# Three transfer edits in an attention-plus-dense kernel: first input block prepared one loop earlier, weight load cut into three, residual loads placed later

## The reference

```
x0: (4, 8192, 1024) float32
xn = layernorm(x0)
# attention part
k, v, q = fft(xn @ Wk.T + bk), fft(xn @ Wv.T + bv), fft(xn @ Wq.T + bq)
kv = cumsum(k * v, axis=1)
a = kv * conj(q);  a = a / (1e-9 + norm(a));  attn = real(ifft(a)) / sqrt(1024)
# dense part, with weights that are +1 or -1 (booleans k0, k1, k2)
h = concat([xn, -xn]) @ w0 * s0;  h = relu(h) * 2
h = h @ w1 * s1;                  h = relu(h) * 2
ffn = h @ w2 * s2
return x0 + attn + ffn
```

## Time and profile before

| what | us |
|---|---|
| median of 2 executions | 4095.31 (4073.11 and 4117.51) |
| profiled execution, device time | 4067.28 |
| its span, slowest core (7) | 4065.5 |
| spans of all cores | 4044.3 to 4065.5 |
| PE busy | 3647.6 (90%) |
| mean granted TensorE clock | 0.950 |

### The profile page before, as it was taken

The page is one execution under the profiler, slowest core; times in us unless marked ns, Lnnn a source line. Parts: engine busy times, 40 slices in busy tenths (PEclk is TensorE's granted clock), DMA queues, the critical chain, the costliest instruction groups (busy, mean ns, idle before and its releaser), DMA issues.

```text
span 4065.5 us, 43732 instructions; the slowest of 8 cores (4044.3 to 4065.5 us)
## 1 busy us (share of the span) xinstructions
PE 3647.6 (90%) x16512; PEld 1590.1 (39%) x16512; DVE 1119.8 (28%) x1586; ACT 1131.4 (28%) x1504; POOL 700.3 (17%) x842
## 2 busy tenths in 40 slices
PE   4658895898994999899899999989989998999998
PEld 1323331333331444344344444434434443444443
DVE  0034436687770111111211301111121111112112
ACT  3844442445553210311211031031112103112110
POOL 0022223455550002001100100100010010001001
PEclk9778897899997999999999999999999999999999
DMA  4143343544415344343434424334443443434343
GB/s 83 21 104 83 84 101 71 88 73 93 84 34 183 106 154 141 122 152 137 143 135 155 157 102 155 133 124 158 155 156 104 156 132 117 155 132 148 125 151 129
DMA packets 331198, 491.53 MB, mean 121 GB/s; under 512 B 217328, under 2 KB 219376, under 8 KB 297200
## 3 DMA queue, kind: packets, MB, share of 16 engines
q0 software_dynamic: 97632, 375.43, 28.2%
q1 hardware_dynamic: 219536, 71.36, 7.9%
q10 hardware_dynamic: 13824, 41.95, 2.8%
HBM read 276.87 MB, written 58.72 MB: 83 GB/s over the span
## 4 chain that ended last, share of the span: by engine, by line
PE 82%; DMA 5%; DVE 4%; issue 4%; ACT 3%; SPq 2%; POOL 0%; ACTq 0%; DVEq 0%; POOLq 0%
PE pd L962 44%; PE pd L661 13%; PE pd L918 11%; PE pd L1018 10%; PE pd L666 2%; PE pd L297 2%; DMA xn_f<-xn_dram 1%; SPq L533 1%; SPq L885 1%; DMA wtmp<-Wk 1%; DVE bx_t L1047 1%; PE pd L504 1%; DVE xn_t L482 1%; DMA xn_dram<-xn_t 1%; DMA w2ring<-k2u 1%
## 5 line engine op out<-in xcount | busy, mean ns | idle before, releaser
L962 PE MATMUL pd<-r_t,w1r 128*128 128x512 bf16 x8192 | 1769.4, 379 | 7.8 <-ACT r_t L932 7.8
L962 PEld LDWEIGHTS pd<-r_t,w1r 128*128 128x128 bf16 x8192 | 801.0, 98 | 976.2 <-issue 11.6
L980 DVE TENSOR_SCALAR w1r<-w1r 128x4096 bf16<-128x4096 bf16 x232 | 284.7, 1227 | 1830.2 <-DMA w1r<-w1s 1830.2
L918 PE MATMUL pd<-xn_f,K0d_t 128*128 128x512 bf16 x2048 | 460.2, 388 | 121.0 <-DMA xn_f<-xn_dram 57.0
L975 POOL DMA_DIRECT2D w1r<-w1s x232 | 125.7, 542 | 2095.5 <-PE pd L962 1830.3
L988 ACT ACTIVATE r_t<-pd,s_scales 128x512 bf16<-128x512 f32 x256 | 176.5, 689 | 1112.4 <-PE pd L962 1111.6
L1018 PE MATMUL pd<-w2ring,r_t 128*128 128x512 bf16 x2048 | 444.7, 379 | 12.3 <-ACT r_t L988 7.8
L918 PEld LDWEIGHTS pd<-xn_f,K0d_t 128*128 128x128 bf16 x2048 | 203.3, 100 | 377.9 <-issue 148.8
L1018 PEld LDWEIGHTS pd<-w2ring,r_t 128*128 128x128 bf16 x2048 | 199.1, 98 | 257.9 <-issue 21.3
L932 ACT ACT_TABLE_LOAD x64 | 82.1, 1283 | 615.0 <-DMA part_t<-partial_dram 506.6
L661 PE MATMUL pd<-xn_f,AkR 128*128 128x512 bf16 x512 | 144.4, 433 | 89.8 <-DMA xn_f<-xn_dram 77.8
(11 more groups left out here) (150 smaller groups left out, 2486.3 us busy)
## 6 DMA issues: line engine op xcount, KB each, us to landing
w1r<-w1s POOLq DMA_DIRECT2D x256, 1024.0 KB, 4.7
w2ring<-k2u POOLq DMA_DIRECT2D x256, 256.0 KB, 2.6
conv_t<-k0u POOLq DMA_DIRECT2D x64, 256.0 KB, 4.0
w1s<-k1u SPq DMA_DIRECT2D x32, 512.0 KB, 5.7
bx_t<-x_own ACTq DMA_DIRECT2D x32, 512.0 KB, 7.3
out<-bx_t ACTq DMA_DIRECT2D x32, 512.0 KB, 3.1
x_t<-x_extra POOLq DMA_DIRECT2D x8, 1024.0 KB, 9.4
k0s<-conv_o SPq DMA_DIRECT2D x32, 256.0 KB, 2.9
```

The source lines that it names most:

```text
L918: inst = te.matmul(reg.ap, K0d_t[:, dk * F0 + m * 128: dk * F0 + (m + 1) * 128], xn_f[fb][:, dk * TST:(dk + 1) * TST], start=(dk == 0), st ...
L962: inst = te.matmul(reg.ap, w1ring[c % 3][:, k * 128:(k + 1) * 128], r0_t[:, k * TST:(k + 1) * TST], start=(k == 0), stop=(k == NF0 - 1))
L980: lambda: v.tensor_scalar(w1ring[c % 3][:], w1ring[c % 3][:], 2.0, -1.0, op0=OP.mult, op1=OP.add))
```

## The change

Three edits, all of when and on which engine something is issued; no arithmetic changes.

1. The preparation of own block 0 is taken out of A2's iteration 0 and put into A1's last iteration (`it` 8), where it runs as the callback of the last projection. The x load that belonged to A2's iteration 0 moves with it.
2. The load of `K0d_t` is cut in three: rows 0 to 2 of 8 on SP, 3 to 5 on ACT, 6 and 7 on POOL; stage 0 waits for all three.
3. The loads of `part_t` and `bx_t` stand behind the last evacuation of stage 1 instead of ahead of stage 0; those of `part_t` stay on ACT, those of `bx_t` are issued by SP.

```
@@ A1 loop
         if it < NST:
             emit_prep_pre(it)
             mid = mk_prep_finish(it, None, None)
+        else:
+            emit_prep_pre(0)
+            mid = mk_prep_finish(0, xn_dram, "xn_dram")
...
         if it < NST:
             emit_next_xload()
+        else:
+            emit_next_xload()
         emit_conv_tasks(4)
@@ A2 loop
-        if it < NST:
+        if 1 <= it < NST:
             emit_prep_pre(it)
             mid = mk_prep_finish(it, xn_dram, "xn_dram")
...
-        if it < NST:
+        if 1 <= it < NST:
             emit_next_xload()
@@ phase B
         barrier(sync, "sp")
-        dstep(sync, "sp", s_k0d, ["k0s"], ["K0d"],
-              lambda: sync.dma_start(K0d_t[:], k0s.ap().rearrange("(k p) m -> p k m", p=128)))
+        dstep(sync, "sp", s_k0d, ["k0s"], ["K0da"],
+              lambda: sync.dma_start(
+                  K0d_t[:, 0:3 * F0],
+                  k0s.ap()[0:3 * 128, :].rearrange("(k p) m -> p k m", p=128)))
...
         barrier(sc, "act")
+        dstep(sc, "act", s_xnw2, ["k0s"], ["K0db"],
+              lambda: sc.dma_start(
+                  K0d_t[:, 3 * F0:6 * F0],
+                  k0s.ap()[3 * 128:6 * 128, :].rearrange("(k p) m -> p k m", p=128)))
...
         barrier(g, "pool")
+        dstep(g, "pool", s_bld, ["k0s"], ["K0dc"],
+              lambda: g.dma_start(
+                  K0d_t[:, 6 * F0:8 * F0],
+                  k0s.ap()[6 * 128:8 * 128, :].rearrange("(k p) m -> p k m", p=128)))
@@ emit_compute_b, ahead of stage 0
-        for tci in range(NTC):
-            @block.scalar
-            def _(sc, j=j, tci=tci):
-                dstep(sc, "act", s_pr[tci], [f"partial_dram{tci}"], [f"bpart{tci}"],
...
-                dstep(sc, "act", s_bx[tci], [], [f"bx{tci}"],
...
-                    dep_wait(te, "pe", fkeys + ["K0d"], [])
+                    dep_wait(te, "pe", fkeys + ["K0da", "K0db", "K0dc"], [])
...
@@ emit_compute_b, behind stage 1
+        for tci in range(NTC):
+            @block.scalar
+            def _(sc, j=j, tci=tci):
+                dstep(sc, "act", s_pr[tci], [f"partial_dram{tci}"], [f"bpart{tci}"],
...
+            @block.sync
+            def _(sync, j=j, tci=tci):
+                dstep(sync, "sp", s_bx[tci], [], [f"bx{tci}"],
...
```

More of the change, by code:

```diff
@@ L894, in emit_compute_b @@
         fb = j % 2
-        for tci in range(NTC):
-            @block.scalar
-            def _(sc, j=j, tci=tci):
-                dstep(sc, "act", s_pr[tci], [f"partial_dram{tci}"], [f"bpart{tci}"],
-                      lambda: sc.dma_start(
-                          part_t[tci][:],
-                          partial_dram.ap()[j * TST + tci * 128: j * TST + (tci + 1) * 128, :]))
-                dstep(sc, "act", s_bx[tci], [], [f"bx{tci}"],
-                      lambda: sc.dma_start(
-                          bx_t[tci][:],
-                          x_own.ap()[j * TST + tci * 128: j * TST + (tci + 1) * 128, :]))
         for g0 in range(0, NF0, 4):
@@ L923, in _ @@
                     v = s_pe.inc(inst)
-                    record(s_pe, v, fkeys + ["K0d"], [])
+                    record(s_pe, v, fkeys + ["K0da", "K0db", "K0dc"], [])
                 pend.append((m, reg, s_pe.n))
@@ L992, in emit_compute_b @@
         r1keys = [f"r1_{c}" for c in range(NF1)]
+        for tci in range(NTC):
+            @block.scalar
+            def _(sc, j=j, tci=tci):
+                dstep(sc, "act", s_pr[tci], [f"partial_dram{tci}"], [f"bpart{tci}"],
+                      lambda: sc.dma_start(
+                          part_t[tci][:],
+                          partial_dram.ap()[j * TST + tci * 128: j * TST + (tci + 1) * 128, :]))
+            @block.sync
+            def _(sync, j=j, tci=tci):
+                dstep(sync, "sp", s_bx[tci], [], [f"bx{tci}"],
+                      lambda: sync.dma_start(
+                          bx_t[tci][:],
+                          x_own.ap()[j * TST + tci * 128: j * TST + (tci + 1) * 128, :]))
         for c in range(4):
```

## The result

The changed kernel took 4038.17 us (median of 13 executions, 4027.12 to 4668.2) where the kernel before took 4068.92 us on the same chip (10 executions, 4060.74 to 4198.69). The ratio is 0.9886 with a 95% interval of 0.9845 to 0.9928: a gain of 46 us, between 29 and 63. That interval is wide: the fastest executions of the two kernels differ by 34 us and the profiled ones by 40. The forecast was a gain of 49 us and 4024 us.

What follows compares the result with a forecast made beforehand. PE was taken as the bound, with gains only where it stands idle: seam 27, weight load 15, borders 8, less 1 for stage 2, make 49 us off 4073.1, so 4024 us; range 4000 to 4069.

Steps and rivals of the forecast that it cites:

- Within 2%: Whole kernel: measured time within 2% (82 us) of no change, chance 0.85; faster 0.12, slower 0.03.
- The seam: Where A1 meets A2: PE idles 8.1 us instead of 35.2, a gain of 27 us, bounds 24 and 35.
- The cover for the eight copies: SP in A2: the `w1s` copies are issued by 658, block 1's store is due at 672; 14 us spare, cost 0.
- the rival in which A2 gives the seam back: A2: block 1's store is delayed or DVE and POOL hold A2; 20 of 27 us return, 4044 us, chance 0.10.
- The borders: Block borders of phase B: PE's stage 0 wait for ACT goes, 8.1 us over six borders, bounds 6 and 9.
- the 1 us put against it: Start of stage 2: `part_t` loads delay the `w2ring` reloads, between 0 and 10 us in all, taken as 1.
- The slower rival: Stage 2: `w2ring` runs dry at each start, 74 us lost against a gain of 50; 4097 us, chance 0.04.
- The weight load: Start of phase B: PE starts at 1278.7 instead of 1293.70, a gain of 15 us by edit 2 and moved loads.
- the lower bound: Weight load at start of phase B: least gain 7 us, from 11.5 MB at 362 GB/s plus 7.7 us of tail.
- My sum by bytes: Start of phase B: K0d, three `w1r` and the transposes, 12.6 MB at 391 GB/s, take 32 us.
- The first rival: Start of phase B: pieces share full engines, transposes issue as late as before; edit 2 brings 7 us, 4032 us, chance 0.20.
- the transposes still land 7 us behind K0d: Start of phase B: a sign named ahead that, if seen in the profile after, makes the forecast wrong.

Runs made afterwards that it cites:

- only_moved: The kernel before with edit 3 alone: K0d whole on SP, `part_t` and `bx_t` loads behind stage 1; 4052.92 us.
- seam_moved: The changed kernel without edit 2: K0d as one load on SP, edits 1 and 3 kept; ratio 0.9932 to the kernel before.
- only_cut: The kernel before with edit 2 alone: K0d in three pieces, `part_t` and `bx_t` loads still ahead of stage 0; 4069.09 us.
- ring_held: The changed kernel with POOL's first three `w1r` loads held until block 0's transposes have landed; 4040.77 us.
- transposes_early: The changed kernel with block 0's eight transposes issued in A2, two iterations before the barrier; 4024.68 us.
- ring_ahead: The changed kernel with the three `w1r` loads ahead of POOL's piece of K0d instead of behind it; 4018.93 us.
- transposes_first: The changed kernel with SP issuing its piece of K0d behind block 0's eight transposes; 4026.19 us.
- ring_late: The changed kernel with POOL's first three `w1r` loads held until all of K0d has landed; 4028.32 us.
- columns_evict: The changed kernel plus transposes in A2, K0d in four column pieces on SP, `w1r` behind, DVE emptying banks 4 to 7 first with early release; ratio 0.9808.
- only_seam: The kernel before with edit 1 alone, edits 2 and 3 taken back; ratio 0.9954 to the kernel before.
- stores_sp: The columns_evict kernel with the four stores of a block issued by SP instead of ACT; 3933.13 and 3943.40 us.

## Why the prediction was right, and where it was wrong

The gain was forecast as 49 us and is 46 us by the ratio, 41.8 us by the terms of the profiled executions and 39.9 by their mean span. That 46 lies so near to 49 is in part luck, as the interval goes from 29 to 63; the terms say more than the total. "Within 2%" was the forecast and is what happened. Term by term:

**The seam, 27 us forecast, 27.1 measured.** The store was let leave at 600 and left at 599.69. The restart was put at 620.2 with 8.1 us idle; it was 618.19 with 6.67. The round trip took 18.5 us and not 20.2. The cover for the eight copies was put at 14 us and measured 8 us (block 1's store at 669.64 less 661.4), since the copies came 6.4 us apart (eight issues in 45.17 us) and not 5.7; it held. A2 stayed at 597.9 us, so the rival in which A2 gives the seam back is refuted.

**The borders, 8 us less 1 us forecast, 7.0 measured.** The wait for ACT is gone, the ring's waits went from 4.5 to 3.9 us and not up, so the 1 us put against it wasn't paid. only_moved repeats the gain without the other edits (6.1 us). The slower rival needed a ring that runs dry in every stage 2, and PE's waits for it are 3.9 us in all.

**The weight load, 15 us forecast, 7.1 measured: this term was mis-sized.** It reached the lower bound only. The weight itself came as reckoned: it was in 28.2 us behind its issue, where the sum had 29.5 for it and `w1r`. The step that failed is "With 3.15 MB on SP's queue instead of 8.39 SP gets them out while the rest of the weight is still coming". SP got two out before the weight was in, and the eighth only 37.6 us behind the K0d issue, 9 us after the weight was in. In only_moved and seam_moved, with the whole weight on SP's queue, it was out after 35.8 and 37.6 us (1258.94 less 1221.39 in seam_moved), and in only_cut after 47.1 against 45.5 before. I had read the 36.6 us of SP's first two issues as the effect of the weight on its own queue. But these pairs show that what stands on SP's queue made a difference of 2 us at most, and not to the good; what shortens SP's stop is less traffic in the window: 9.5 us of the start went with the moved loads, and in ring_held, without `w1r`, the eighth was out after 30.3 us. My sum by bytes also priced the transposes at 1.05 MB, 2.7 us; transposes_early shows that they hold 13.6 us.

The first rival, the cut without use, had edit 2 and its window at 7 us and the forecast at 4032. It named the right mechanism and nearly the right figure, and I gave it 0.20. Its sum of 41 us meets the 41.8 of the terms better than my 49. Even it was too kind to the cut, since 9.5 us come from the loads that edit 3 moved (only_moved) and the cut takes 2.4 of them back. ring_ahead shows by what: `w1r` behind POOL's piece. In the Trainium skill the page DMA: Bandwidth & Descriptors, section Issuing engines are not separate DMA queues, says that a DMA from SP, ACT or POOL ends up on the same 16 engines and that more issuers save only the time of issuing. Start 49.4 against 48.2 us in only_cut agrees. That the later loads of the third issuer fall behind is what ring_ahead adds.

Of the checks named ahead, "the transposes still land 7 us behind K0d" was to make the forecast wrong, and they landed 13 us behind. Total and range still held, since the term was 15 of 49 us and the other terms were right to 1 us.

Open is why transposes beside full engines cost five times their bytes (13.6 us against 2.7). transposes_first, ring_late and ring_held show only that SP stands long in each order, not why.

## What to carry to other kernels

Sum a start by the bytes in its window, but price DMA transposes apart: take them out of the window altogether (13.6 us here for 1 MB), instead of changing which queue the bulk load stands in. When a load must be waited for, cut it along the axis in which the first consumer reads it (41.1 to 9.1 us together with that and with the next loads held back), and not along the axis of its issuers; and look at what the added issue pushes back on its engine. When one wait is removed at a border, look for the DMA issues that wait for a late result ahead of the next evacuation: columns_evict won 15 us, and moving the four stores of each block 46 us more.

## What the runs showed of the hardware

**DMA transposes and a bulk load.** While the weight came, SP's eighth transpose was out 35.8 to 37.6 us behind the K0d issue whether 8.39 MB stood on SP's own queue (only_moved, seam_moved) or 3.15 MB (the changed kernel). Only the place of the stop differed: 15.80 and 12.41 us at the first two transposes in only_moved, 1.14, 21.30 and 6.26 at the first three in the changed kernel. With five eighths of the weight and `w1r` beside them SP needed 30 us to issue the eight (transposes_first), with none of that 11.33 us (the seam above).

**Two cores of a pair at the seam at once.** In the kernels with edit 1, the pairs 0/1, 2/3, 4/5 and 6/7 reach the seam at their own times. In 6 pairs of 44 the two cores came within 1.6 us of one another. Their idle time there was 9.9 to 11.6 us instead of 6.3 to 9.0, and their A2 600 to 607 us instead of 594 to 602. Two of the six are in only_seam, which is why it shows 21.9 us and not 27. The Trainium skill's HBM Reference, section Specifications (TRN2), says that the two cores of a pair share one memory's bandwidth. That would fit; no run here separates it from other causes, so it is argued and not shown.

**The granted clock after a stop at a border.** The first 32 matmuls of block 1's stage 0, before and in columns_evict, and those behind columns_evict's second stop:

```profile
1637.35:1646.32 8.97, 8.97 (x32) 3.53 (x32) 5.68 (x5) 0.67 (x1) 0.00 (x0) 0.78 0.63 207
1572.20:1579.28 7.08, 7.07 (x32) 3.02 (x32) 6.87 (x6) 0.00 (x0) 0.00 (x0) 1.00 0.56 216
1583.65:1590.00 6.35, 6.35 (x24) 2.65 (x25) 0.73 (x1) 4.15 (x6) 0.00 (x0) 0.79 0.87 320
```

Before, after 8.00 us idle, the granted clock is 0.78 in this stretch (in its first 3.65 us it is 0.50, the 1.2 GHz level) and the matmuls take 8.97 us. In columns_evict, after 1.61 us idle, it is 1.00, the 2.4 GHz level, and they take 7.07 us; but after the second stop of 4.38 us it is 0.79. So columns_evict kept a mean of 388 ns in stage 0, and only stores_sp, whose borders have the short stop alone, has 380 ns (busy 445.0 us against 460.3). That is 15 us of the 46 us that stores_sp has over columns_evict; 30.6 us are ACT's wait.
